# The reciprocal row scales of a convolution's output, spread over the partitions through DRAM in place of a diagonal and a product with ones

## What is computed

```python
def fake_quant(t, axis):
    s = jnp.max(jnp.abs(t), axis=axis, keepdims=True) / QMAX
    s = jnp.maximum(s, 1e-08)
    return jnp.clip(jnp.round(t / s), -QMAX - 1.0, QMAX) * s
def qlinear(x, w):
    return jnp.einsum('bsh,oh->bso', fake_quant(x, -1), fake_quant(w, 1))

y = irfft(rfft(x, 2048) * rfft(K, 2048))[..., :1024] + x * D[:, None]
y = y * (arange(1024) < length[:, None])[:, None, :]
h = silu(qlinear(y, w_gate)) * qlinear(y, w_up)      # 1024 -> 2752
out = x + qlinear(h, w_down)                         # 2752 -> 1024
```

## Time and profile before

| | |
|---|---|
| median of 2 runs | 1320.66 us (1317.04 to 1324.29) |
| profiled execution | 1316.23 us |
| its span, first to last instruction | 1313.0 us |
| mean granted TensorE clock | 0.996 |
| PE busy | 1242.5 us (95%) |
| DVE busy | 915.2 us (70%) |
| ACT, POOL busy | 408.7, 339.5 us |
| convolution stage, first to last scaling of y (L790) | 83.2 to 398.3 us |
| feed-forward stage, from its first product | 403.15 us to the end |

### The profile page before, as it was taken

The page is one execution under the profiler, slowest core; times in us unless marked ns, Lnnn a source line. Parts: engine busy times, 40 slices in busy tenths (PEclk is TensorE's granted clock), DMA queues, the critical chain, the costliest instruction groups (busy, mean ns, idle before and its releaser), DMA issues.

```text
span 1313.0 us, 19670 instructions
## 1 busy us (share of the span) xinstructions
PE 1242.5 (95%) x6581; PEld 675.8 (51%) x6676; DVE 915.2 (70%) x1542; ACT 408.7 (31%) x595; POOL 339.5 (26%) x318
## 2 busy tenths in 40 slices
PE   2499999999997999999999999999999999999997
PEld 0377777776763444444444444444444444444443
DVE  7578888888876577765677755677756677756675
ACT  2244454445531322222322222222222222222222
POOL 2133344325530321121221121221121221122220
PEclk9999999999998999999999999999999999999999
DMA  3279999998962233322223322323322323322322
GB/s 100 86 227 283 288 278 296 290 300 251 305 211 83 43 72 78 86 62 70 69 69 78 86 62 70 70 68 81 83 62 70 70 68 83 81 62 70 70 63 78
DMA packets 137593, 161.51 MB, mean 123 GB/s; under 512 B 101644, under 2 KB 101854, under 8 KB 136286
## 3 DMA queue, kind: packets, MB, share of 16 engines
q1 hardware_dynamic: 137566, 161.16, 45.3%
HBM read 113.28 MB, written 25.49 MB: 106 GB/s over the span
## 4 chain that ended last, share of the span: by engine, by line
PE 68%; issue 0%; DVE 0%; ACT 0%
PE ps_g L1055 23%; PE ps_u L1055 23%; PE ps_o L1081 22%; PE ps_o L1088 1%; PE ps_t L1065 0%; ACT h_t L1190 0%; DVE ps_o L1142 0%; DVE res L1145 0%
## 5 line engine op out<-in xcount | busy, mean ns | idle before, releaser
L1219 POOL TENSOR_TENSOR h_int<-h,rounder 128x512 bf16<-128x512 f32 x186 | 174.4, 952 | 703.3 <-ACT h L1181 700.6
L1055 PE MATMUL ps_g<-wgu,rows 128*128 128x512 bf16 (+1 forms) x1516 | 327.1, 358 | 5.9 <-PEq L405 4.9
L1055 PE MATMUL ps_u<-wgu,rows 128*128 128x512 bf16 (+1 forms) x1493 | 324.7, 357 | 2.3
L1081 PE MATMUL ps_o<-wd,h_t 128*128 128x512 bf16 x1314 | 294.0, 379 | 1.8 <-issue 0.2
L1175 ACT ACTIVATE g_buf<-g_buf 128x512 f32<-128x512 f32 x192 | 112.3, 585 | 584.1 <-DVE g_buf L1113 584.1
L1113 DVE SCALAR_TENSOR_TENSOR g_buf<-ps_g,sx_all,wide 128x512 f32<-128x512 f32 x192 | 132.3, 689 | 229.6 <-PE ps_g L1055 229.6
L846 PE MATMUL ps_y<-u,toep 128*128 128x512 f32 (+7 forms) x1024 | 266.2, 413 | 2.3 <-ACT s_rows L715 0.9
L1055 PEld LDWEIGHTS ps_g<-wgu,rows 128*128 128x128 bf16 x1536 | 145.2, 98 | 163.5 <-issue 13.2
L1055 PEld LDWEIGHTS ps_u<-wgu,rows 128*128 128x128 bf16 x1536 | 147.1, 98 | 151.8 <-issue 1.4
L846 PEld LDWEIGHTS ps_y<-u,toep 128*128 128x128 f32 x1024 | 177.6, 192 | 89.6 <-issue 57.5
L1081 PEld LDWEIGHTS ps_o<-wd,h_t 128*128 128x128 bf16 x1346 | 131.0, 98 | 151.9 <-issue 1.1
(11 more groups left out here) (140 smaller groups left out, 623.1 us busy)
## 6 DMA issues: line engine op xcount, KB each, us to landing
toep<-k_rev SPq DMA_DIRECT2D x64, 512.0 KB, 6.4
res<-in_x SPq DMA_DIRECT2D x64, 256.0 KB, 3.9
out_x<-res SPq DMA_DIRECT2D x64, 256.0 KB, 3.2
wide<-in_L_ffn_w_gate SPq DMA_DIRECT2D x22, 512.0 KB, 6.8
wide<-in_L_ffn_w_up SPq DMA_DIRECT2D x22, 512.0 KB, 8.7
wide<-in_L_ffn_w_down SPq DMA_DIRECT2D x8, 1376.0 KB, 7.5
rows<-in_x SPq DMA_DIRECT2D x32, 256.0 KB, 6.8
x_more<-in_x SPq DMA_DIRECT2D x32, 256.0 KB, 7.0
```

The lines of the kernel that those rows point to most:

```text
L1055: last = pe.matmul(bank[:, 0:n], xq[:, par, c, :], wgu[:, NC - 1 - c, first + cols.start:first + cols.stop], start=(c == 0), stop=(c == NC ...
L1081: last = pe.matmul(ps_o[o][:], h_t[0:width, c, :], wd[0:width, c, o * W:(o + 1) * W], start=(c == 0), stop=(c == FC - 1))
L1219: pool.tensor_tensor(h_int[:, piece(j)], h[:, par, piece(j)], rounder[:].to_broadcast([P, n]), ALU.subtract).then_inc(h_int_ready, 1)
```

## The change

`t_inv` is no longer put on a diagonal. SP stores it in a row of a new DRAM tensor `inv_dram`, waits until the store has landed, and loads the row back with a source that is the same for all 128 partitions, into `inv_row` in SBUF. `quantise_y` waits for that load and takes `inv_row` in place of `ps_i`. DVE waits for the landing of the previous store before it writes `t_inv` again. The diagonal, PE's product and the PSUM tile are gone. All three new steps of SP stand ahead of `store_xq`.

```diff
@@ convolve_and_pack
-        diag = sb("diag", [P, P])
+        inv_row = sb("inv_row", [P, P])
-        ps_i = psum("ps_i", [P, P])
@@ SP, body
                 if not isinstance(i, int) or i >= 1:
+                    spread_inv(i - 1)
                     store_xq(i - 1)
                 if has(i, TILES - 2):
                     sp.wait_ge(conv_done, 2 * i + 2)
                     load_t(i + 2, par, 1)
                 if isinstance(i, int) and i == TILES - 1:
+                    spread_inv(i)
                     store_xq(i)
+
+            def spread_inv(i):
+                sp.wait_ge(inv_ready, i + 1)
+                sp.dma_start(inv_dram[bass.ds(i, 1), :].rearrange("a p -> p a"), t_inv[:]).then_inc(inv_stored, 16)
+                sp.wait_ge(inv_stored, 16 * i + 16)
+                sp.dma_start(inv_row[:], inv_dram[bass.ds(i, 1), :].to_broadcast([P, P])).then_inc(inv_spread, 16)
@@ DVE, scale_y and quantise_y
-                dve.reciprocal(t_inv[:], t_s[:]).then_inc(scale_step, 1)
+                if not isinstance(i, int) or i >= 1:
+                    dve.wait_ge(inv_stored, 16 * i)
+                dve.reciprocal(t_inv[:], t_s[:]).then_inc(inv_ready, 1)
                 dve.tensor_copy(sx_all[:, bass.ds(i, 1)], t_s[:]).then_inc(scale_step, 1)
-                dve.wait_ge(scale_step, 4 * i + 4)
-                dve.tensor_scalar(diag[:], ident[:], t_inv[:], None, ALU.mult).then_inc(diag_ready, 1)
...
-                dve.wait_ge(inv_spread, i + 1)
+                dve.wait_ge(inv_spread, 16 * i + 16)
-                dve.tensor_tensor(v, v, ps_i[:].unsqueeze(1).to_broadcast([P, NC, P]), ALU.mult).then_inc(y_scaled, 1)
+                dve.tensor_tensor(v, v, inv_row[:].unsqueeze(1).to_broadcast([P, NC, P]), ALU.mult).then_inc(y_scaled, 1)
@@ PE
-            def spread_inv(i):
-                pe.wait_ge(diag_ready, i + 1)
-                pe.matmul(ps_i[:], ones[:], diag[:], start=True, stop=True).then_inc(inv_spread, 1)
```

More of the change, by code:

```diff
@@ L390, in _, with convolve_and_pack @@
                     last[hp].then_inc(k_done, 1)
-def convolve_and_pack(nc, d, x, w_gate, w_up, w_down, k_rev, xq_dram, s_dram, ident, ones, identb, rounder, mask,
+def convolve_and_pack(nc, d, x, w_gate, w_up, w_down, k_rev, xq_dram, s_dram, inv_dram, ident, ones, identb, rounder, mask,
                       wgu, wd, sx_all, w_f32, toep, x_bufs, t_loaded, x_loaded, w_loaded):
@@ L443, in convolve_and_pack @@
         scale_step = sem("scale_step")
-        diag_ready = sem("diag_ready")
+        inv_ready = sem("inv_ready")
+        inv_stored = sem("inv_stored")
         inv_spread = sem("inv_spread")
@@ L773, in scale_y @@
                 dve.tensor_reduce(t_max[:], ps_m[:], X, ALU.max).then_inc(scale_step, 1)
-                dve.wait_ge(scale_step, 4 * i + 1)
+                dve.wait_ge(scale_step, 3 * i + 1)
                 dve.tensor_scalar(t_s[:], t_max[:], 1.0 / QMAX, S_MIN, ALU.mult, ALU.max).then_inc(scale_step, 1)
-                dve.wait_ge(scale_step, 4 * i + 2)
-                dve.reciprocal(t_inv[:], t_s[:]).then_inc(scale_step, 1)
+                dve.wait_ge(scale_step, 3 * i + 2)
+                if not isinstance(i, int) or i >= 1:
+                    dve.wait_ge(inv_stored, 16 * i)
+                dve.reciprocal(t_inv[:], t_s[:]).then_inc(inv_ready, 1)
                 dve.tensor_copy(sx_all[:, bass.ds(i, 1)], t_s[:]).then_inc(scale_step, 1)
-                dve.wait_ge(scale_step, 4 * i + 4)
-                dve.tensor_scalar(diag[:], ident[:], t_inv[:], None, ALU.mult).then_inc(diag_ready, 1)
             def max_y(i, par):
@@ L868, in turn_max @@
                 pe.transpose(ps_m[:], y_max[:], ident[:]).then_inc(max_turned, 1)
-            def spread_inv(i):
-                pe.wait_ge(diag_ready, i + 1)
-                pe.matmul(ps_i[:], ones[:], diag[:], start=True, stop=True).then_inc(inv_spread, 1)
             def turn_scales(first, n, at, steps):
-                pe.wait_ge(diag_ready, at)
+                pe.wait_ge(inv_ready, at)
                 pe.wait_ge(w_step, steps)
@@ L895, in body @@
                             turn_w(i, par, 1)
[L896 to L900, removed]
+                    if hh == 0 and (not isinstance(i, int) or i >= 1):
+                        turn_max(i - 1)
                 if isinstance(i, int) and i == GU_ITERS:
@@ L909, in _ @@
             turn_max(TILES - 1)
-            spread_inv(TILES - 1)
 def tile_slots(rows, chunks):
@@ L1235, in build @@
     xq_dram = nc.dram_tensor("xq_dram", [d["TILES"], P, d["L"]], BF16).ap()
+    inv_dram = nc.dram_tensor("inv_dram", [d["TILES"], P], F32).ap()
     s_dram = nc.dram_tensor("s_dram", [3, d["F"]], F32).ap()
@@ L1262, in build @@
                          scratch, x, w_gate, w_up, wide, toep, x_bufs, t_loaded, x_loaded, w_loaded)
-            convolve_and_pack(nc, d, x, w_gate, w_up, w_down, k_rev, xq_dram, s_dram, ident, ones, identb, rounder, mask,
+            convolve_and_pack(nc, d, x, w_gate, w_up, w_down, k_rev, xq_dram, s_dram, inv_dram, ident, ones, identb, rounder, mask,
                               wgu, wd, sx_all, wide, toep, x_bufs, t_loaded, x_loaded, w_loaded)
```

## The result

The changed kernel takes 1717.0 us (median of 2 runs, 1717.02 to 1717.05) against 1320.66 before. The ratio is 1.3035, 95% interval 1.2958 to 1.3111. That is slower, as forecast, but by 396 us and not by 165, and it lies outside the range of 1425 to 1545.

A forecast was written before the change was run, and what follows sets the result against it. PE and the DMA queue were both taken as full. Periods of 15.9 us with gate and up weights, up to 16.1 with down weights, summed over the stage to +165 us on 1316.2; with 4.4 for the median, 1486 us, range 1425 to 1545.

The forecast's parts named there:

- The bound: Convolution stage: PE and the DMA queue both full, PE busy 10.06 of 10.06 us, DMA share 1.01.
- the ring: Per tile: scaling of y, loads, small store's landing, broadcast load's landing, next scaling; period from 10.1 to 15.9 us.
- the small transfers that pass the queue: Rival: store and load not held up by the whole queue, 2.4 to 3.2 us each; 1355 to 1400 us; chance 0.08.
- the hidden spread: Rival: both transfers fit between reciprocal and scaling of y, nothing lost; 1307 to 1312 us, or 1335; chance 0.04.
- The burst: The tile's whole traffic in SP's queue: 10.0 us of transfer, landed 13.3 us after the scaling of y starts (D).
- The failed step: Small store of reciprocals to DRAM: lands right behind the loads ahead of it, 0.2 us taken, bounds 0 to 1.0.
- The constant of about 2.0 us: Skill's rule of constant cost per transfer, mostly landing notice; by it alone two transfers some 4.2 us, sum about +14 us.
- The second mis-sized term: Load of 128 rows of 512 bytes after the store lands, into an empty queue: 2.2 us, bounds 1.7 to 3.2.
- the prediction's own 3.85 us: Time per tile from the end of the reciprocal to the scaling of y, available for both transfers in sequence.
- The clock: Rival: TensorE's clock falls while PE idles; hidden unless all PE work runs at 1.2 GHz, then some 1600 us; chance 0.04.
- The removal: Diagonal on DVE (0.29 us) and two PE passes (0.44 us) per tile gone: 9 to 14 us gained if PE stayed limiting.

The follow-up runs named there:

- the run that was to take it away: Kernel before without diagonal and product, y multiplied by ones, plus a DVE wait for POOL's first weight conversion before rounding y: 1366 us, ratio 1.0397.
- the cheapest way through DRAM that was tried: Changed kernel with a one-piece 512-byte store of ones, and store, wait and broadcast load all ahead of the tile's weight and x loads: 1427 us, ratio 1.0857.

## Why the prediction was wrong

**The bound and the ring were right.** The queue was full, the small store landed behind the up load that was issued ahead of it, and SP's and DVE's waits closed the ring that was described. DVE idles for 382.6 us ahead of the scaling, always until the broadcast load. The feed-forward stage is unchanged. Of the rivals, the small transfers that pass the queue are ruled out by the store's 12.3 us, and the hidden spread by the same.

**The burst was nearly right.** It landed at D+13.95 against D+13.3.

**The failed step is the store's landing: "The nearest, the 64 scales of the earlier trace rows, added nothing that can be seen, and I bound it by 0 and 1.0 us. I take 0.2."** It measured 5.1 us (315.70 to 320.80), with no transfer to be seen in the DMA engines. Those scales lay side by side in one partition and went out as one run of bytes. `t_inv` has one value in each of 128 partitions and goes out as 128 pieces of 4 bytes into one row. The step took a row with another form of transfer for the nearest and set an upper bound that no row supported. The runs showed in its place: one piece, or pieces 64 bytes apart, stay about within the bounds of 0 and 1.0 us; 128 adjacent pieces add 5 us, hold up what is queued behind them, and take hardly less in another queue. A bare store of this form, at the end of the stage, takes 8.4 us (787.67 to 796.09) where a 256 KB store took 2.0. In it the pieces are out of the DMA engines before 789, and no packet follows until 796. The constant of about 2.0 us that the prediction names beside its sum doesn't hold for this form either. Why neighbours cost so much is open.

**The second mis-sized term is the broadcast load: 2.2 us taken, 3.2 as the upper bound, 4.3 measured.** The row nearest in form, the broadcast with 3.2 us, was set aside because the queue is empty. With an ordinary source it is 2.8 us. The other 1.4 us come with reading what the pieces have just written.

Together with the burst's 0.65 these give the 7.5 us by which a tile exceeds the forecast (23.4 against 15.9), 218 us over 29 steps, which is most of the 231 us missing.

Three sums of the prediction are off by a little. The upper bounds add up to a period of 18.0 us, not 17.8, which doesn't reach 23.4 either. By the prediction's own 3.85 us the two transfers of 4.2 us would cost about 11 us, not 14. The chances give 0.96 for slower by over 2%, not 0.95.

**The clock** fell as the rival said it might, to 0.72 on average in a tile, and was nearly hidden as argued. The part of that rival that would have set the pace did not come. **The removal** was put at nothing while PE waits, and at 9 to 14 us if PE stayed the bound. The second figure isn't borne out: without any spread the kernel is 1% slower and not 9 to 14 us faster. The rows show DVE's rounding and scaling falling on POOL's conversions there, with 45 us more of DVE's time in sum. That this is the whole cause is argued, as the run that was to take it away didn't.

No version tried here beats the kernel before. The diagonal and the product take 0.44 us of PE and 0.29 of DVE per tile, and the cheapest way through DRAM that was tried cost 8.6%.

## What to carry to other kernels

A store from [128 partitions, 1 element] into one DRAM row is 128 pieces. Price it from a measured transfer of the same form, or measure it by itself; here the number of bytes said nothing. Before a wait for a landing is put on the engine that issues all transfers, look at the DMA share. Where it was 1.00, as here, each such wait emptied the queue, and the loads made ahead didn't help. When an operation is taken out, look at what the next ones now run beside. A diagonal and a product with ones on an engine that has the data at hand were cheap next to two landings.

## What the runs showed of the hardware

- A store of 128 adjacent pieces of 4 bytes lands 5.1 us after the burst ahead of it, and 8.4 us after its issue with an almost empty queue. With 64 bytes between their starts the store lands in 7.5 us behind the burst, the same as with 512 bytes (7.6). With 64 adjacent pieces it is 10.8, with 128 it is 12.0. The pieces are out of the DMA engines within about a microsecond (packets of 9 ns), and the time lies between that and the notice. Why neighbours hurt, and why not in proportion, is open.
- Packets of 4 KB queued behind such a store took 2.6 to 3.0 us in place of 0.16.
- Reading back the row just written in pieces takes 4.2 us, the same row written in one piece 2.8.
- DVE's rounding of 128x1024 f32 from and to SBUF takes 0.69 us alone. Begun under an operation of POOL with two tensors it takes what is left of that operation plus 0.55 us, 2.17 as the median without a spread. The Trainium skill (GPSIMD Engine Reference, Specifications) says that the SBUF interfaces of POOL are shared with DVE and contend with DVE's two-port modes and with its instructions that have two inputs in SBUF, and these rows agree. The scaling shows it too: with its factor in SBUF it takes what is left plus 1.08 us, 2.29 as the median of the last version through DRAM. With the factor in PSUM it was at 1.21 to 1.22 in all 32 tiles before.
